# Iterated feed-forward stage: row statistics finished for two groups at a time, and one centred tile that alternates between ScalarE and GpSimd

## The reference, cut to what matters

```python
def step(h, _):
    h = h + 0.01 * jnp.tanh(h)
    h = h * jax.nn.sigmoid(h)
    h = _layernorm(h, ln_w, ln_b)      # (h - mean) * rsqrt(var + 1e-5) * w + bias, per row of 128
    h = jnp.einsum('bsc,dc->bsd', h, W) + b
    return (h, None)
x, _ = jax.lax.scan(step, x, None, length=30)
```

## Time and profile before

| | us |
|---|---|
| median of 3 runs | 1299.74 (1299.24 to 1300.05) |
| the profiled execution, its own time | 1298.93 |
| its span (first to last instruction) | 1297.2 |
| iterated stage with all engines in step, 620 to 1220 us | 600 |

### The profile page before, as it was taken

How to read it: one execution, slowest core, us unless ns; L and a number is a source line. 1 busy time by engine, 2 the same in 40 slices (tenths; PEclk the granted TensorE clock), 3 DMA queues, 4 the chain that set the end, 5 groups by cost and what they waited for, 6 DMA issues and landing times.

```text
span 1297.2 us, 29539 instructions
## 1 busy us (share of the span) xinstructions
PE 1259.5 (97%) x9309; PEld 1123.3 (87%) x9309; DVE 1192.2 (92%) x2807; ACT 1003.6 (77%) x1408; POOL 961.8 (74%) x783
## 2 busy tenths in 40 slices
PE   8899999999999999689999999999999999999998
PEld 7677777777777777489999999999999999999998
DVE  7888888888888876899999999999999999999997
ACT  2455555555555554689999999999999999999995
POOL 3455555545555554399999999999999999999995
PEclk9999999999999999889999999999999999999999
DMA  6111111111111000000000000000000000000004
GB/s 191 41 42 42 46 55 55 47 40 40 40 40 40 0 1 1 1 2 0 0 0 0 0 0 0 0 0 0 0 0 0 0 0 0 0 0 0 0 0 130
DMA packets 29792, 27.71 MB, mean 21 GB/s; under 512 B 3269, under 2 KB 21448, under 8 KB 29640
## 3 DMA queue, kind: packets, MB, share of 16 engines
q1 hardware_dynamic: 29768, 27.41, 6.8%
HBM read 23.21 MB, written 4.19 MB: 21 GB/s over the span
## 4 chain that ended last, share of the span: by engine, by line
PE 83%; DVE 11%; issue 3%; ACT 2%; DMA 0%; POOL 0%; SPq 0%; DVEq 0%; ACTq 0%; POOLq 0%
PE psum L843 33%; PE psum L857 16%; PE psum L839 7%; PE psum L614 4%; PE psum L616 4%; PE psum L615 4%; PE psum L785 4%; PE psum L636 3%; PE psum L631 3%; DVE emb_n L1332 2%; DVE xh_mem L1190 1%; PE psum L625 1%; ACT emb_f L961 1%; PE psum L645 1%; DVE upd L1295 1%
## 5 line engine op out<-in xcount | busy, mean ns | idle before, releaser
L479 POOL TENSOR_TENSOR f_rs<-f_var,half_neg 128x8 f32<-128x8 f32 x240 | 396.6, 1653 | 28.6 <-DVE f_var L1248 10.4
L915 ACT ACTIVATE g_ring<-u_ring 128x1024 f32<-128x1024 f32 x240 | 392.6, 1636 | 3.0 <-DVE u_ring L1239 3.0
L843 PEld LDWEIGHTS psum<-w_t,y_all 128*128 128x128 f32 x2880 | 382.7, 193 | 9.3
L843 PE MATMUL psum<-w_t,y_all 128*128 128x128 f32 x2880 | 388.6, 275 | 0.0
L939 ACT ACTIVATE y_all<-psum 128x1024 f32<-128x1024 f32 x240 | 382.6, 1594 | 7.1 <-PE psum L857 7.0
L924 ACT ACTIVATE t_ring<-psum 128x1024 f32<-128x1024 f32 x232 | 373.7, 1611 | 3.2 <-PE psum L843 3.2
L1223 DVE BATCH_NORM_STATS2 f_stat<-g_ring 128x6 f32<-128x256 f32 x960 | 341.0, 415 | 0.1
L483 POOL TENSOR_TENSOR h_ring<-g_ring,f_rs 128x640 f32<-128x640 f32 x240 | 303.0, 1262 | 18.8
L1239 DVE SCALAR_TENSOR_TENSOR u_ring<-t_ring,psum 128x1024 f32<-128x1024 f32 x232 | 278.4, 1200 | 0.0
L857 PE MATMUL psum<-ident,h_ring 128*128 128x128 f32 (+1 forms) x1920 | 251.5, 274 | 7.4 <-DVE h_ring L1210 7.4
L857 PEld LDWEIGHTS psum<-ident,h_ring 128*128 128x128 f32 (+1 forms) x1920 | 231.5, 154 | 8.0 <-issue 8.0
(11 more groups left out here) (192 smaller groups left out, 2138.4 us busy)
## 6 DMA issues: line engine op xcount, KB each, us to landing
work<-in_adj_dram SPq DMA_DIRECT2D x16, 1024.0 KB, 5.5
x_tok<-in_x_dram SPq DMA_DIRECT2D x16, 256.0 KB, 5.6
out_dram<-y_all SPq DMA_DIRECT2D x8, 512.0 KB, 3.2
work<-in_L_gnn_conv_w_dram SPq DMA_DIRECT2D x1, 1088.0 KB
work<-in_L_gnn_w_ih_dram SPq DMA_DIRECT2D x1, 384.0 KB
work<-in_L_gnn_w_hh_dram SPq DMA_DIRECT2D x1, 192.0 KB
work<-in_L_gnn_W_dram SPq DMA_DIRECT2D x1, 64.0 KB, 5.2
work<-in_L_ffn_weight_dram SPq DMA_DIRECT2D x1, 64.0 KB, 4.8
```

Of the source, the lines that this page charges most:

```text
L479: pool.tensor_tensor(f_rs[:, j % 4, :], f_var[:, j % 2, :], half_neg[:, 0:GT], ALU.pow).then_inc(f_pow, 1)
L843: m = pe.matmul(y_ps[k % 2][:, h, C * t:C * t + C], y_all[:, GT * k + NT * h + t, :], w1_t[:] if t < biased else w1c_t[:], start=False, st ...
L915: act.activation(g_ring[j], u_ring[j % 2], ACT.Silu).then_inc(f_silu, 1)
```

## The change

Statistics are finished for a pair of groups (an even one and the odd one behind it). VectorE's reduction (now L1261) runs only in the slots of odd groups, for 16 tiles at once, and `LAG_V` becomes 2; GpSimd's power (now L484) runs on 16 values per partition, once per pair, and `LAG_P` becomes 3. Behind it GpSimd does the even group's 5 tiles, one new small instruction, and the odd group's 6 tiles (all in one slot, every other slot). ScalarE handles a tile only in even groups, and now centres it there: it computes `rs*g - mean*rs`, with `-mean*rs` made by the new GpSimd instruction (`f_nmr`, L493, semaphore `f_nm`). So the even group has 3 centred tiles and the odd one 2, and the bias matmul of an even group's second half covers 1 tile and not 2.

```diff
-LAG_V = 3
-LAG_P = 4
+LAG_V = 2
+LAG_P = 3
-ACT_TILES = (1, 1, 1, 1, 1, 1, 1, 1)
+ACT_TILES = (1, 0, 1, 0, 1, 0, 1, 0)
 DVE_TILES = (2, 2, 2, 2, 2, 2, 2, 2)
+CENTRED = tuple(a + d for a, d in zip(ACT_TILES, DVE_TILES))
...
             def slot(it, k):      # GpSimd
                 before = earlier(it, k, LAG_P)
-                if before is None:
+                if before is None or before[1] % 2 == 0:
                     return
                 i, j, s = before
+                pair = (j // 2) % 2
                 pool.wait_ge(f_v, s + 1)
                 wait(pool, f_norm_act, act_norms(i, j + 1) - sum(ACT_TILES) // 2)
-                pool.tensor_tensor(f_rs[:, j % 4, :], f_var[:, j % 2, :], half_neg[:, 0:GT], ALU.pow).then_inc(f_pow, 1)
+                pool.tensor_tensor(f_rs[:, 2 * pair:2 * pair + 2, :], f_var[:, pair, :, :],
+                                   half_neg[:].rearrange("p (g t) -> p g t", g=2), ALU.pow).then_inc(f_pow, 2)
                 pool.wait_ge(f_pow, s + 1)
-                wait(pool, f_turn, s - 3)
-                t = GT - ACT_TILES[j] - DVE_TILES[j]
-                pool.tensor_tensor(tiles(h_ring[j % 4])[:, 0:t, :], tiles(g_ring[j])[:, 0:t, :],
-                                   spread(f_rs[:, j % 4, 0:t], t, C), ALU.mult).then_inc(f_norm, 1)
+                for g in (j - 1, j):
+                    wait(pool, f_turn, s - 4 + g % 2)
+                    t = GT - CENTRED[g]
+                    pool.tensor_tensor(tiles(h_ring[g % 4])[:, 0:t, :], tiles(g_ring[g])[:, 0:t, :],
+                                       spread(f_rs[:, g % 4, 0:t], t, C), ALU.mult).then_inc(f_norm, 1)
+                    if g < j:
+                        pool.tensor_scalar(f_nmr[:, pair:pair + 1], f_stat[:, 2 * pair, 0, t, 1:2], f_rs[:, 2 * pair, t:t + 1], -1.0,
+                                           ALU.mult, ALU.mult).then_inc(f_nm, 1)
...
-                    centred = GT - DVE_TILES[k]      # TensorE, bias matmul
+                    centred = GT - CENTRED[k]
...
-                    act.wait_ge(f_pow, s + 1)        # ScalarE
+                    act.wait_ge(f_nm, act_norms(before[0], j + 1))
...
-                        ins = act.activation(tiles(h_ring[j % 4])[:, t, :], tiles(g_ring[j])[:, t, :], ACT.Copy,
-                                             scale=f_rs[:, j % 4, t:t + 1])
+                        ins = act.activation(tiles(h_ring[j % 4])[:, t, :], tiles(g_ring[j])[:, t, :], ACT.Identity,
+                                             bias=f_nmr[:, (j // 2) % 2:(j // 2) % 2 + 1], scale=f_rs[:, j % 4, t:t + 1])
...
                     wait(dve, f_v, s - 3)            # VectorE, ahead of bn_stats
+                    if j % 2 == 0:
+                        wait(dve, f_nm, act_norms(i, j) - 1)
...
-                if before is not None:               # VectorE, reduction
+                if before is not None and before[1] % 2 == 1:
                     _, j, s = before
+                    pair = (j // 2) % 2
                     dve.wait_ge(f_bn, s + 1)
-                    wait(dve, f_pow, s - 1)
-                    squares = f_stat[:, j % 4, :, :, 2].rearrange("p o t -> p t o")
-                    dve.tensor_reduce(f_var[:, j % 2, :], squares, AX_X, ALU.add).then_inc(f_v, 1)
+                    wait(dve, f_pow, s - 3)
+                    squares = f_stat[:, 2 * pair:2 * pair + 2, :, :, 2].rearrange("p g o t -> p g t o")
+                    dve.tensor_reduce(f_var[:, pair, :, :], squares, AX_X, ALU.add).then_inc(f_v, 2)
```

More of the change, by code:

```diff
@@ L97, in build @@
         bias1 = sb("bias1", [KB, NT, C], BF16)
-        half_neg = sb("half_neg", [P, 8])
+        half_neg = sb("half_neg", [P, 2 * GT])
         f_stat = sb("f_stat", [P, 4, 2, GT, 3])
-        f_var = sb("f_var", [P, 2, GT])
+        f_var = sb("f_var", [P, 2, 2, GT])
+        f_nmr = sb("f_nmr", [P, 2])
         f_rs = sb("f_rs", [P, 4, GT])
@@ L282, in build @@
         f_v = sem("f_v")
+        f_nm = sem("f_nm")
         f_pow = sem("f_pow")
@@ L854, in slot @@
                     for t in range(GT):
-                        rows = P if t < GT - DVE_TILES[j] else P - 1
+                        rows = P if t < GT - CENTRED[j] else P - 1
                         m = pe.transpose(g_ps[j % 2][0:rows, t // NT, P * (t % NT):P * (t % NT) + P],
@@ L1215, in slot @@
                 if before is not None:
-                    _, j, s = before
+                    i, j, s = before
                     dve.wait_ge(f_silu, s + 1)
                     wait(dve, f_v, s - 3)
+                    if j % 2 == 0:
+                        wait(dve, f_nm, act_norms(i, j) - 1)
                     wait(dve, f_norm_dve, s - 3)
@@ L1304, in step @@
                     for r in range(2):
-                        ins = dve.memset(g_ps[r][3 * QUAD:P, 1, C * (NT - DVE_TILES[r]):], 1.0)
+                        ins = dve.memset(g_ps[r][3 * QUAD:P, 1, C * (NT - CENTRED[r]):], 1.0)
                     ins.then_inc(s_ones, 1)
```

## The result

| | us |
|---|---|
| before, median (4 runs) | 1299.49 (1297.86 to 1300.05) |
| changed, median (4 runs) | 1446.65 (1446.13 to 1447.89) |
| ratio | 1.1138, 95% interval 1.1125 to 1.1151 |
| profiled execution, its own time and span | 1446.13, 1444.2 |

The change costs 147 us, 1.23 us for each of the 120 pairs. I had forecast 1322 us, 22 us slower: the direction was right and the size far too small.

The account below looks back on a forecast made before the run. VectorE was taken as the bound before, at 6.12 us per pair; a loop through power, GpSimd and ScalarE would make it 6.31. 0.19 us for 120 pairs, 22 us, gave 1322 us, range 1308 to 1336.

Parts of the forecast that it names:

- loop 1: Once per pair, reduction through power and even group's tiles to next reduction: 6.24 us; as sole limit 1314 us, chance 0.18.
- a VectorE slot without the reduction: Last term of loop 1 and loop 2: VectorE's work from the centred tiles to the next reduction, 2.98 us.
- loop 2: Once per two pairs, reduction through power, GpSimd, ScalarE and back to VectorE: 12.61 us, 6.31 per pair, chance 0.58.
- 0.4 as a sign: Expected in the profile: ScalarE idle ahead of its tile, released by GpSimd's small instruction, about 0.4 us per pair.
- VectorE as the bound of before: Claim that in the kernel before VectorE waits for nobody and fills its slot of 3.06 us.
- the slack of 1.20 us: Time between the power's end and its first user before; the longer power was to lose 1.24 us against it.
- the way from reduction to power: Reduction 0.18 us plus hand-over from VectorE to GpSimd's power 0.16 us, at the start of both loops.
- Small terms: Sizes taken for GpSimd's small instruction, sixth tile, reduction, power-to-tiles step and ScalarE's tile: 0.19, 1.51, 0.18, 0.07, 0.39 us.
- The rival of a full GpSimd: GpSimd's own work plus waits becomes the bound, about 6.4 us per pair: 34 us slower, 1334 us, chance 0.13.
- The rival of a gain by fewer VectorE instructions: VectorE's own work stays the bound and loses 0.07 us per pair: 8 us faster, 1291 us, chance 0.06.

Follow-up runs that it names:

- e_nmfirst: The changed kernel with the small f_nmr instruction ahead of the even group's five tiles on GpSimd, nothing left out: 1331.59 us, ratio to before 1.0251.
- e_small: The changed kernel with GpSimd's tile products cut from 5 and 6 tiles to one each, the others left out: 1344.68 us, ratio to before 1.0351.
- e_b_last: The kernel before with VectorE's two centred tiles moved behind u, into the five-tile product: 1412.32 us, ratio 1.0876.
- e_pair: The changed kernel with the old tile split (one reduction and power per pair, no f_nmr): 1477.94 us, ratio to before 1.1377.
- e_late: e_nmfirst with VectorE's centred tiles moved behind bn_stats in its slot, 1.35 us later: 1464.42 us, ratio to before 1.1269.
- e_b_mid: The kernel before with VectorE's two centred tiles moved behind bn_stats, ahead of u: 1299.38 us, ratio 1.0004.
- e_two: e_pair with two powers of 8 values, one per group, then the two five-tile products: 1296.30 us, ratio to before 0.9984.
- e_stt: The changed kernel with VectorE's centred tiles written as scalar_tensor_tensor, same result: 1458.42 us, ratio to before 1.1226.
- e_two_split: e_two with the odd group's centred tiles moved behind bn_stats in their slot: 1302.26 us, ratio to before 1.0028.

## Why the prediction was wrong, point by point

- **The step that failed** is in loop 1, "a VectorE slot without the reduction, 3.06 - 0.08 = 2.98". It took the even group's tiles at their undisturbed 0.51 us, from the earlier trace rows. In the changed kernel they take 1.46 us (1.55 in every fourth pair) and the term is 3.91. The same term stands in loop 2, so both sums lacked it. e_nmfirst shows it: with the product 0.3 us later and all work kept the term is 2.98 again and 115 us are gone. e_small, e_b_last, e_pair and e_late show it from other sides. Of the 1.27 us that a pair became longer, VectorE's held tiles are 0.97 and its idle time behind the power 0.29.
- The row that would have told me was in my own groups. In the earlier trace rows the two tiles are recorded at 1.64 us beside 0.61 in the earlier trace rows; I read its 0.16 us of idle time and not its duration; a product started 0.04 us behind the tiles there (1283.67). The same lies at the stage's start, in before's trace, in order of time:

```profile
559.32 1.21 DVE L1239 SCALAR_TENSOR_TENSOR u_ring<-t_ring,y_all 128x1024 f32<-128x1024 f32 x1
559.38 2.27 POOL L483 TENSOR_TENSOR h_ring<-g_ring,f_rs 128x640 f32<-128x640 f32 x1
560.45 0.17 DVE L1248 TENSOR_REDUCE f_var<-f_stat 128x8 f32<-128x16 f32 x1
560.53 1.46 DVE L1210 TENSOR_SCALAR h_ring<-g_ring,f_stat,f_rs 128x128 f32<-128x128 f32 x2
```

  Both directions stand in four rows: a `u` with both inputs in SBUF delays the product by 1.0 us (2.27 for 1.26), and the product then holds the tiles until it ends (559.38 + 2.27 = 561.65).
- The Trainium skill (SBUF — State Buffer, section SBUF: two separate sides) has this as a rule that I didn't weigh: VectorE and GpSimd share one pair of ports as an exclusive lock; VectorE takes it for an instruction in a two-port mode or with two SBUF inputs, and whoever comes second fully blocks. The rows agree on the tiles in both forms (1.46 and 1.61 us) and on `bn_stats` and `u` from PSUM, which ran beside products undisturbed. They agree that a tile which is first holds the product: in the changed kernel it is recorded at 1.34 us behind a first tile, for 1.26. They differ on its taking any GpSimd instruction, for all of its length: the power let tiles through in e_b_mid, and there the measurement decides. That a `tensor_scalar` tile runs in a two-port mode is shown by no run here.
- "Loop 2 is the longer one and sets the time": wrong. e_pair has no `f_nmr` and is slower still. ScalarE did wait for it, 132.3 us in all, 1.36 us a pair where I had named 0.4 as a sign, but VectorE has no idle time ahead of `bn_stats` (L1235: 0.0). In the pair shown the silu ended at 907.77 (906.73 + 1.04), ahead of the `bn_stats` at 908.15: the wait cost nothing.
- VectorE as the bound of before: right, and so is the argument of the slack of 1.20 us against a longer power. The power became longer by 1.35 us (3.0 for 1.65) and not 1.24, and in e_nmfirst VectorE stands idle behind it, 0.28 us a pair; this is what its 32 us are. Loop 1 was put at 6.24 us, 14 us; it is 6.44 without the collision. Mis-sized were the power, 3.0 for 2.88, and the way from reduction to power, 0.43 for 0.34. (120 x 0.32 would be 38 us; where the other 6 us are was not followed.)
- Small terms: `f_nmr` 0.264 for 0.19, the sixth tile 1.47 for 1.51, the reduction 0.192 for 0.18, GpSimd from power to product 0.16 for 0.07, ScalarE's tile 0.40 (905.43 to 905.83) for 0.39. None of them matters.
- The rival of a full GpSimd (1334 us) is not what happened: GpSimd stands idle 122.2 / 98 = 1.25 us ahead of each power. The rival of a gain by fewer VectorE instructions had a true core: in e_two the reductions take 0.06 us less of a pair, which would be the 8 us, but the tiles take 0.05 us more, and 2 us are left. Why the tiles do was not followed.

## What to carry to other kernels

Before moving work between VectorE and GpSimd, or moving a release, look in order of time at which of their instructions overlap, and compare the same instruction in different neighbourhoods, by its duration and by the distance to the next start: where both are sometimes 0.5 us and sometimes 1.5, it may be kept out, and no idle time shows it. Two engines released by the same semaphore start together; where they can't run together, put a short instruction or the other work of one of them first. When results of two steps are batched, ask when the first user needs the first half: with one power of 16 values the even group's result came 1.4 us later than with two powers of 8.

## What the runs showed of the hardware that I had not expected

- VectorE's instruction on SBUF tiles, short as it is (0.25 us), is kept out by a GpSimd tile product until its end: 1.46 us for two tiles instead of 0.51, with one product. Where two products follow each other directly, one tile gets through between them and the next is held again: 2.0 us for two in e_late, 2.5 in every fourth pair of e_pair.
- A tenth of a microsecond decides who comes first: a tile whose recorded start was 0.12 us ahead of the product's got through in every pair, one 0.02 to 0.04 us ahead was held in every pair (the changed kernel, e_small, e_pair and e_stt, the whole stage).
- A GpSimd power on 8 values doesn't do that in 1.7 us of running (e_b_mid), and `bn_stats` and a `u` that reads PSUM are not held by a product: 414 and 1200 ns in the changed kernel, 415 and 1199 before.
- The power is 0.155 to 0.17 us for each value, and by that an estimated 0.4 us of start: 0.700, 1.02, 1.64 and 3.0 us for 2, 4, 8 and 16 values.
- The steady order of these engines sits in windows of 0.1 to 0.2 us: in e_two the odd tiles start that far behind the end of a product in 96 of 98 pairs, e_two_split hits one in 7 pairs of 97 and is 6 us slower than e_two.
